# A new order of the four engines inside a quad of the attention, and wider column tiles in the recurrence's output matmuls

## The chip, the cores and the metric

The kernel runs on one core of a Trainium2 chip. The metric is the device time of one execution in microseconds (us). The kernel before takes 2658.96 us, the median of three runs (2658.64 to 2659.07).

## The reference

The program is one layer of a hybrid model on a stream of 2 x 2048 tokens with 256 features. It adds four blocks to the stream, each behind a layer norm:

```
x = x + attn_a(norm(x));  x = x + ffn(norm(x));  x = x + attn_b(norm(x));  x = x + ffn(norm(x))

# attn_a, 16 heads of 16 dims, segments of 64 tokens
scores = q k^T / 4, causal
out_t  = softmax(scores in the own and the previous segment) v        # the "window"
att    = softmax(scores)
pcs    = sum of att over the 64 rows of a segment, each row times exp(index_decay)
w      = decayed running sum of pcs over the segments before, divided by its sum + 1e-5
kv     = for each segment: sum over tokens s of  w[s] * k[s] (outer) v[s]
y      = sigmoid(mix) * out_t + (1 - sigmoid(mix)) * (q kv);   y @ Wc^T

# attn_b: tokens are routed to 2 of 4 memories (1024 tokens kept in each); a gated linear recurrence
# S = S * exp(g_t) + k_t v_t ;  o_t = q_t S   runs over each memory and over all tokens (shared)
# ffn: 16 experts, top 2, and a shared expert
```

## The kernel before, in words

The program is a row of phases. The change touches two: `phase_attend` (the softmax attention of attn_a, about 130 to 1240 us of the trace) and `phase_gla` (the recurrence of attn_b, about 1742 to 2292 us).

**phase_attend.** There are 2 x 16 = 32 heads (index n), and each head has 16 tiles of 128 query rows (t). A head is worked in four quads (q = 0 to 3) of four tiles: q, 7 - q, 8 + q and 15 - q; g = 4 n + q counts the quads, 128 in all. A quad's scores are made in units: unit 0 is the masked window (`window`, 768 columns), and units 1 to 4 or 1 to 5 are the causal score blocks (`scores(g, k)`), each up to 1024 columns in one of three PSUM buffers S. The quads q = 0 and q = 3 have four score units, q = 1 and q = 2 have five. Every unit goes through the engines in this order: TensorE writes S; VectorE takes the row minimum (`window_minima`, L725; `minima`, L737 and L740); ScalarE takes the exponential into SBUF (`window_exps`, L656; `exps`, L666). A fourth unit can only be written when the exponential of the first of the three has ended (TensorE's wait on `s_E`).

From the exponentials of quad g two chains run while the units of quad g + 1 are made.

- The window chain uses one PSUM bank M: TensorE turns the window (`turned`, L864); VectorE copies it to SBUF (`keep_transposed`, L757); TensorE multiplies it by v (`values`, L880); VectorE divides it and writes it to the stream (`outputs`, L764 and L767). Only then may M be written again.
- The share chain: GpSimd takes the difference of each block's minimum to the row's (`differences`, L556), ScalarE its exponential (`factors`, L673), GpSimd sums the window's diagonal part (`diag_sums`, L584 to L593) and the row totals (the first half of `weights`, L564 to L568), VectorE inverts them (`inverses`, L751), and GpSimd makes the shares c2 (the second half of `weights`, L570 and L576), in two buffers. TensorE uses c2(g) as stationary operand in `sums` (L887), which adds the column sums of quad g into the PSUM bank pcs in the next iteration.

Behind a head's last quad the sums of that head go on, spread over the next head's quads: ScalarE copies pcs to SBUF (`keep_pcs`, L679); TensorE turns it into M at the end of iteration q = 1 (`turn_pcs`, L922); ScalarE copies that (`keep_pcsT`, L685); TensorE multiplies it by the outer products kvo, in two halves (`products`, L933), one at the end of q = 2 and one behind the window of q = 3; ScalarE copies the result (`keep_kvr`, L691); TensorE applies the decay (`decayed`, L942), and VectorE normalises (`normalise`, L775 to L781). GpSimd makes kvo (`products`, L605) in parts of 5, 5 and 6 tiles in its iterations q = 3, 0 and 1. All of these use M too, so `turned` waits for `keep_pcsT` in q = 2, for `keep_kvr` in q = 3 and for `normalise` in q = 0.

Each engine's order is written out by hand: the loops over g at the end of each engine's block. An engine runs its list strictly in order, so an instruction that waits holds back all behind it.

**phase_gla.** 24 iterations of four chains of 128 tokens. TensorE computes the output of a pair of chains in `output(i, p)` (48 calls): for each of two chains a product of the queries with the state spread over 256 columns (`gl_bd`, L2670), and for each of four heads a product of the masked scores A with V, 64 columns (L2675). Both are cut into strips of output rows, `STRIP = P // 4 = 32` rows, so that the four strips lie in the four column groups of the array and their records (two for each f32 product) start nearly together.

Of the kernel before, what the change touches and what calls it, by code (L numbers as in the profile page):

```python
# [13 lines left out]
P = 128  # L14
# [3 lines left out]
NT = L // P  # L18
# [401 lines left out]
NQ = 4  # L420
# [5 lines left out]
def phase_attend(nc, q_parts, k_parts, k_tok, v_tok, tw, eid, decay, sq, sk, kh, vh, vs, ident, identb, mask, Y, kv_dram, x, q_full, wc, kvc,  # L426
                 q0, x0, wc_s, own, state, keep):

    with ExitStack() as ctx:
# [3 lines left out]
        NHEAD = B * H  # L433
        NG = NHEAD * NQ
# [111 lines left out]
        def _(pool):  # L546
# [7 lines left out]
            def differences(g):  # L554
                pool.wait_ge(s_top, g + 1)
                pool.tensor_tensor(diff[:, g % 2, :, :], mn[:, g % NQ, :, :],  # L556
                                   top[:, g % 2, :].unsqueeze(2).to_broadcast([P, NQ, KK]), ALU.subtract
                                   ).then_inc(s_diff, 1)

            def weights(g):  # L560
                q = g % NQ
                pool.wait_ge(s_f, g + 1)
                pool.wait_ge(s_ds, g + 1)
                pool.tensor_tensor(fr[:, :, :], f[:, q, :, :], rs[:, q, :, :], ALU.mult).then_inc(s_w, 1)  # L564
                pool.wait_ge(s_w, 3 * g + 1)
                pool.tensor_tensor(tot2[:, :], fr[:, :, 0], fr[:, :, 1], ALU.add).then_inc(s_w, 1)
                pool.wait_ge(s_w, 3 * g + 2)
                pool.tensor_tensor(tot[:, g % 2, :], tot2[:, :], fr[:, :, 2], ALU.add).then_inc(s_tot, 1)  # L568
                pool.wait_ge(s_inv, g + 1)
                pool.tensor_tensor(fi[:, :, :], f[:, q, :, :], inv[:, g % 2, :].unsqueeze(2).to_broadcast([P, NQ, KK]),  # L570
                                   ALU.mult).then_inc(s_w, 1)
                pool.wait_ge(s_w, 3 * g + 3)
                if g >= 2:
                    pool.wait_ge(s_P, g - 1)
                h = g // NQ % H
                pool.tensor_tensor(c2[:, g % 2, :, :, PAD:PAD + 2],  # L576
                                   fi[:, :, :].unsqueeze(3).to_broadcast([P, NQ, KK, 2]),
                                   eid[:, h, :].unsqueeze(1).unsqueeze(1).to_broadcast([P, NQ, KK, 2]),
                                   ALU.mult).then_inc(s_c2, 1)
# [32 lines left out]
            diag_sums(0)  # L612
            for g in range(NG):
                n, q = divmod(g, NQ)
                weights(g)
                if q == 3:
                    products(n, 0, 5)
                elif n and q == 0:
                    products(n - 1, 5, 10)
                elif n and q == 1:  # L620
                    products(n - 1, 10, NT)
                if g + 1 < NG:
                    differences(g + 1)
                    diag_sums(g + 1)
            products(NHEAD - 1, 5, NT)
            pool.memset(own[:, :, :], 1.0).then_inc(s_own, 1)
            pool.wait_ge(s_own, 1)
# [17 lines left out]
        def _(act):  # L645
# [50 lines left out]
            for g in range(NG):  # L696
                n, q = divmod(g, NQ)
                if g + 1 < NG:
                    window_exps(g + 1)
                    if n and q == 3:  # L700
                        keep_kvr(n - 1)
                    last = len(units[(g + 1) % NQ])
                    for k in range(1, 1 + last):
                        exps(g + 1, k)
                        if k == 1:
                            factors(g)
                        if n and k == 4 and q == 0:
                            keep_pcs(n - 1)
                        if n and k == 5 and q == 1:
                            keep_pcsT(n - 1)  # L710
            keep_kvr(NHEAD - 2)
            factors(NG - 1)
            keep_pcs(NHEAD - 1)
            keep_pcsT(NHEAD - 1)
# [3 lines left out]
        def _(dve):  # L718
# [68 lines left out]
            for g in range(NG):  # L787
                n, q = divmod(g, NQ)
                if g + 1 == NG:
                    inverses(g)  # L790
                    keep_transposed(g)
                    outputs(g)
                    if n:
                        normalise(n - 1)
                    break
                window_minima(g + 1)
                for k in range(1, 1 + len(units[(g + 1) % NQ])):
                    minima(g + 1, k)
                    if k == 2:
                        keep_transposed(g)  # L800
                    if k == 3:
                        inverses(g)
                        outputs(g)
                tops(g + 1)
                if n and q == 3:
                    normalise(n - 1)
            dve.wait_ge(s_keep, 1)
            normalise(NHEAD - 1)

# [1 line left out]
        def _(pe):  # L811
# [111 lines left out]
                                               start=True, stop=True)  # L923
                ins.then_inc(s_pT, 1)

            def products(n, part):
                if part == 0:
                    pe.wait_ge(s_pTs, n + 1)
                    pe.wait_ge(s_kvo, n + 1)
                    pe.wait_ge(s_Y, min(n * NQ + NQ + 3, NG))  # L930
                for t in range(part * NT // 2, (part + 1) * NT // 2):
                    j = t % 4
                    ins = nc.tensor.matmul(M[j * R:(j + 1) * R, 0:KVW],  # L933
                                           pcsT[:, t // 4 * P + j * R:t // 4 * P + (j + 1) * R], kvo[:, t, :],
                                           start=(t < 4), stop=(t >= NT - 4))
                if part == 1:
                    ins.then_inc(s_KV, 1)

            def decayed(n):
                pe.wait_ge(s_kvr, n + 1)  # L940
# [3 lines left out]
            window(0)  # L944
            for k in range(1, 1 + len(units[0])):
                scores(0, k)
            def next_sums(g, s, parts):
                if g >= 1:
                    sums(g - 1, s, parts)

            def next_scores(g, k):
                if g + 1 < NG and k <= len(units[(g + 1) % NQ]):
# [2 lines left out]
            for g in range(NG):  # L955
                n, q = divmod(g, NQ)
                if g + 1 < NG:
                    window(g + 1)
                if n and q == 3:
                    products(n - 1, 1)  # L960
                next_sums(g, 0, (0, 1))
                next_scores(g, 1)
                turned(g)
                next_scores(g, 2)
                next_sums(g, 1, (0, 1))
                next_sums(g, 2, (0,))
                next_scores(g, 3)
                values(g)
                next_sums(g, 2, (1,))
                next_scores(g, 4)  # L970
                next_sums(g, 3, (0, 1))
                next_scores(g, 5)
                if n and q == 1:
                    turn_pcs(n - 1)
                if n and q == 2:
                    products(n - 1, 0)
                if n and q == 3:
                    decayed(n - 1)
            for s, parts in ((0, (0, 1)), (1, (0, 1)), (2, (0, 1)), (3, (0, 1))):
                sums(NG - 1, s, parts)  # L980
            turn_pcs(NHEAD - 1)
            products(NHEAD - 1, 0)
            products(NHEAD - 1, 1)
            decayed(NHEAD - 1)


# [1055 lines left out]
def phase_gla(nc, gx, hT_dram, wq, wk, wv, w12, bg, yb, o_dram, ident, later, won, wo, nw):  # L2042

    with ExitStack() as ctx:
# [2 lines left out]
        UP = U * P  # L2047
        BK = 64
        BH = BK // 2
        STRIP = P // 4  # L2050
        NCHUNK = CAP // P
        NG = NCHUNK * (B + 1)
        NSTATE = B * NM + B
# [1019 lines left out]
```

## Time and profile before

| | us |
|---|---|
| median of 3 runs | 2658.96 |
| the profiled execution | 2684.99 |
| its span | 2683.3 |
| TensorE matmul busy | 2124.7 (79%) |
| VectorE busy | 1836.9 (68%) |
| ScalarE busy | 1561.9 (58%) |
| GpSimd busy | 1531.6 (57%) |

The profiled execution is 1.0% longer than the median of the runs. Busy times are those of the whole program; the phases have different limits, so the rows below take one phase or one head at a time. A line of the trace gives start, duration, engine, line of the kernel and operation, and in square brackets how long the engine had been idle and what released it. The duration of a block of matmuls includes the tail of its last record, which overlaps the next block.

### The profile page before, as it was taken

Reading aid. Unit: us, or ns where it says so; the run is one execution under the profiler, and the core shown is the slowest. Engines: PE = TensorE matmul, PEld = TensorE weight load, DVE = VectorE, ACT = ScalarE, POOL = GpSimd, SP = SyncE. Lnnn points to the kernel's source line nnn. Section 1 sums busy time; section 2 is a strip of 40 time slices with the busy share of each in tenths; the row PEclk is TensorE's granted clock in tenths of the full one; section 3 lists DMA queues with packets and bytes.
Section 4 is the critical chain, followed back from the end, with each engine's and each line's share of the span. In section 5 each row is a group of like instructions: output and inputs, shape, how many; then the busy total and the mean of one; then the engine's idle time right before and its main releaser. Section 6 shows DMA issues by size and latency. Waiting matters only on the chain. (4 is left out here: it accounts for less than half of the span.)

```text
span 2683.3 us, 111106 instructions
## 1 busy us (share of the span) xinstructions
PE 2124.7 (79%) x45872; PEld 1600.7 (60%) x45872; DVE 1836.9 (68%) x4507; ACT 1561.9 (58%) x3824; POOL 1531.6 (57%) x3168
## 2 busy tenths in 40 slices
PE   8788888888888888888868944389999998687793
PEld 5456566566566665556637734366766776565682
DVE  6578888887878887884544555276777777575456
ACT  5577777777777777772433322266666665454231
POOL 3357666666766666768554546544444444256452
PEclk9889999999999999999988965699999999789897
DMA  6911111111121111113346654301111111542546
GB/s 216 265 33 40 40 40 40 40 40 40 41 63 39 40 40 40 40 29 120 138 113 209 197 172 153 109 22 47 51 50 51 49 41 35 199 169 89 154 146 225
DMA packets 188851, 245.89 MB, mean 92 GB/s; under 512 B 41672, under 2 KB 144981, under 8 KB 187456
## 3 DMA queue, kind: packets, MB, share of 16 engines
q1 hardware_dynamic: 161824, 182.08, 22.7%
q0 software_dynamic: 19872, 50.41, 5.5%
q8 instruction: 368, 6.03, 0.9%
q10 hardware_dynamic: 6656, 6.31, 0.8%
q14 instruction: 131, 1.07, 0.1%
HBM read 136.08 MB, written 106.50 MB: 90 GB/s over the span
## 5 line engine op out<-in xcount | busy, mean ns | idle before, releaser
L666 ACT ACTIVATE at_E<-at_S,at_mn 128x1024 f32<-128x1024 f32 (+7 forms) x704 | 594.2, 847 | 211.3 <-DVE at_mn L737 178.2
L737 DVE TENSOR_REDUCE at_mn<-at_S 128x1 f32<-128x1024 f32 (+3 forms) x448 | 494.0, 1104 | 152.6 <-PE at_S L846 152.3
L846 PE MATMUL at_S<-am_sk,am_sq 96*32 96x512 bf16 (+3 forms) x4608 | 395.8, 350 | 1.1 <-ACT at_Tt L656 1.0
L887 PE MATMUL at_pcs<-at_E,at_c 128*32 128x256 f32 (+1 forms) x4864 | 375.7, 338 | 0.0
L605 POOL TENSOR_TENSOR at_kvo<-am_kh,am_vh 128x256 f32<-128x256 f32 x512 | 304.2, 628 | 0.0
L887 PEld LDWEIGHTS at_pcs<-at_E,at_c 128*32 128x32 f32 x4864 | 229.7, 109 | 41.2 <-issue 0.2
L1360 POOL DMA_INDIRECT expert_out<-m_ysb,m_dst x158 | 155.5, 984 | 139.3 <-issue 76.7
L887 PE MATMUL at_pcs<-at_Tt,at_c 128*32 128x128 f32 x1024 | 189.8, 274 | 42.3 <-ACT at_pcs_s L679 42.3
L590 POOL TENSOR_TENSOR at_half<-at_half 128x128 f32<-128x128 f32 (+4 forms) x640 | 185.6, 290 | 50.1
L864 PE MATMUL at_M<-am_ident,at_Tt 128*32 128x64 f32 x8192 | 154.5, 225 | 68.9 <-ACT at_kvr L691 43.1
L656 ACT ACTIVATE at_Tt<-at_S,at_mn 128x192 f32<-128x192 f32 x512 | 174.1, 428 | 48.3 <-DVE at_mn L725 48.1
L864 PEld LDWEIGHTS at_M<-am_ident,at_Tt 128*32 128x32 f32 x8192 | 136.3, 112 | 109.0 <-ACT at_Tt L656 54.8
L846 PEld LDWEIGHTS at_S<-am_sk,am_sq 96*32 96x32 bf16 x4608 | 173.8, 97 | 28.8 <-ACT at_Tt L656 10.3
L1672 PE MATMUL m_b<-m_wgu,m_xT 128*128 x632 | 169.1, 391 | 2.3 <-issue 2.0
L2609 PEld LDWEIGHTS gl_S<-gl_X,gl_Y 32*64 32x64 f32 x8448 | 110.5, 133 | 89.3 <-issue 68.9
L2609 PE MATMUL gl_S<-gl_X,gl_Y 32*64 32x32 f32 (+1 forms) x8448 | 132.0, 226 | 38.5 <-issue 24.3
L725 DVE TENSOR_REDUCE at_mn<-at_S 128x4 f32<-128x768 f32 x128 | 121.8, 951 | 34.6 <-PE at_S L829 34.4
L1413 ACT ACTIVATE m_sg<-m_b 128x128 f32<-128x128 f32 x158 | 43.9, 278 | 172.8 <-issue 105.9
L666 ACT ACTIVATION_READ_ACCUMULATOR at_E<-at_S,at_mn 128x1 f32 x704 | 143.0, 203 | 0.0
L887 PEld LDWEIGHTS at_pcs<-at_Tt,at_c 128*32 128x32 f32 x1024 | 107.0, 110 | 60.0 <-issue 48.7
L1672 PEld LDWEIGHTS m_b<-m_wgu,m_xT 128*128 128x128 f32 x632 | 120.2, 195 | 26.0 <-issue 9.9
L2241 POOL DMA_INDIRECT expert_out<-gl_ysb,gl_dst x64 | 64.8, 1013 | 109.7 <-ACT gl_ysb L2357 97.5
(393 smaller groups left out, 5579.9 us busy)
## 6 DMA issues: line engine op xcount, KB each, us to landing
m_xg<-expert_rows SPq DMA_DIRECT2D x158, 129.0 KB
am_sq<-q_parts SPq DMA_DIRECT2D x192, 64.0 KB, 2.3
am_sk<-k_parts SPq DMA_DIRECT2D x192, 64.0 KB, 2.3
memory_rows<-m_blank SPq DMA_DIRECT2D x16, 516.0 KB
gl_hx<-memory_rows SPq DMA_DIRECT2D x32, 258.0 KB, 3.6
m_wgu<-in_f_wgu SPq DMA_DIRECT2D x2, 4096.0 KB
rt_yin<-expert_out SPq DMA_DIRECT2D x7, 1024.0 KB, 11.4
fn_yin<-expert_out SPq DMA_DIRECT2D x7, 1024.0 KB, 8.9
```

The source lines that it names most:

```text
L590: pool.tensor_tensor(half[:, :, 0:w], half[:, :, 0:w], half[:, :, w:2 * w], ALU.add).then_inc(s_half, 1)
L605: ins = pool.tensor_tensor(kvo[:, t, 0:DH * DH].rearrange("p (d e) -> p d e", d=DH), k3[:, t, :].unsqueeze(2).to_broadcast([P, DH, DH]), v ...
L656: ins = nc.scalar.activation(Tt[:, q, s, :], S[v % NS_B][:, at:at + TW], ACT.Exp, bias=mn[:, q, s, 0:1], scale=-1.0)
L666: ins = nc.scalar.activation(E[:, at:at + w], S[v % NS_B][:, i * CW:i * CW + w], ACT.Exp, bias=mn[:, q, s, 1 + j:2 + j], scale=-1.0, accum ...
L725: nc.vector.tensor_reduce(mn[:, g % NQ, :, 0].rearrange("p (b s) -> p b s", b=2), S[v % NS_B][:, :].rearrange("p (b c) -> p b c", b=2)[:, ...
L737: nc.vector.tensor_reduce(mn[:, q, :, :].rearrange("p s k -> p (s k)")[:, at[0]:at[0] + 1], S[v % NS_B][:, 0:w], AX.X, ALU.min).then_inc(s ...
L846: ins = nc.tensor.matmul(S[v % NS_B][x, at:at + cw], sq[:, u, t * P + x.start:t * P + x.stop], sk[:, u, c0 + c:c0 + c + cw], start=True, s ...
L864: ins = nc.tensor.matmul(M[x, s * P + e * SEG:s * P + (e + 1) * SEG], Tt[:, q, s, e * SEG + x.start:e * SEG + x.stop], ident[:, e * SEG:(e ...
L887: ins = nc.tensor.matmul(pcs[j * R:(j + 1) * R, cols[0]:cols[1]].rearrange("p (b c) -> p b c", c=P), lhsT, rhs, start=(n, j) not in touche ...
L1360: pool.indirect_dma_start(out=yb.rearrange("t (j d) -> (t j) d", j=TOPK), out_offset=bass.IndirectOffsetOnAxis(ap=dst[:, t, :], axis=0), i ...
L1672: ins = nc.tensor.matmul(bank[4 + t % 2][:, 0:2 * MH], xT[:, t % 2, k, :], wgu[:, k, ds(at, D)], start=(k == 0), stop=(k == KC - 1))
L2609: return nc.tensor.matmul(out, Y[r_h, i % 2, l, u * P + keys:u * P + keys + out.shape[0]], queries, start=True, stop=True)
```

## The change

On GpSimd `weights` is cut in two, `totals` and `shares`. The order of an iteration g was weights(g), products, differences(g + 1), diag_sums(g + 1); it becomes totals(g), diag_sums(g + 1), shares(g), differences(g + 1), products.

On ScalarE `factors(g)` comes before the first score unit instead of behind it; `keep_pcs` comes behind the last unit of q = 0 instead of the fourth, `keep_pcsT` behind the fourth of q = 1 instead of the fifth, and `keep_kvr` behind the last unit of q = 2 instead of behind the window of q = 3.

On VectorE `keep_transposed` comes behind unit 1 instead of 2, `inverses` behind unit 4 instead of 3, and `normalise` behind unit 4 of q = 3 instead of behind `tops`.

On TensorE the sums of quad g - 1 move back: s = 0 from before `scores(g + 1, 1)` to behind `scores(g + 1, 2)`, s = 1 from there to behind `values`, and the second part of s = 3 to the next iteration, behind its window. `products` is one block of 16 tiles at the end of q = 2, and `decayed` comes before a fifth unit (q = 3 has none).

In `phase_gla` STRIP is 64 instead of 32.

```diff
@@ GpSimd
+            def shares(g):
+                q = g % NQ
                 pool.wait_ge(s_inv, g + 1)
...
-                weights(g)
+                totals(g)
+                if g + 1 < NG:
+                    diag_sums(g + 1)
+                shares(g)
+                if g + 1 < NG:
+                    differences(g + 1)
                 if q == 3:
                     products(n, 0, 5)
...
-                if g + 1 < NG:
-                    differences(g + 1)
-                    diag_sums(g + 1)
@@ ScalarE
                     window_exps(g + 1)
-                    if n and q == 3:
-                        keep_kvr(n - 1)
+                    factors(g)
                     last = len(units[(g + 1) % NQ])
                     for k in range(1, 1 + last):
                         exps(g + 1, k)
-                        if k == 1:
-                            factors(g)
-                        if n and k == 4 and q == 0:
+                        if n and k == last and q == 0:
                             keep_pcs(n - 1)
-                        if n and k == 5 and q == 1:
+                        if n and k == 4 and q == 1:
                             keep_pcsT(n - 1)
+                        if n and k == last and q == 2:
+                            keep_kvr(n - 1)
@@ VectorE
-                    if k == 2:
+                    if k == 1:
                         keep_transposed(g)
                     if k == 3:
+                        outputs(g)
+                    if k == 4:
                         inverses(g)
-                        outputs(g)
+                    if n and k == 4 and q == 3:
+                        normalise(n - 1)
                 tops(g + 1)
-                if n and q == 3:
-                    normalise(n - 1)
@@ TensorE
                     window(g + 1)
-                if n and q == 3:
-                    products(n - 1, 1)
-                next_sums(g, 0, (0, 1))
+                sums_of(g - 2, 3, (1,))
                 next_scores(g, 1)
                 turned(g)
                 next_scores(g, 2)
-                next_sums(g, 1, (0, 1))
-                next_sums(g, 2, (0,))
+                sums_of(g - 1, 0, (0, 1))
+                sums_of(g - 1, 2, (0,))
                 next_scores(g, 3)
                 values(g)
-                next_sums(g, 2, (1,))
+                sums_of(g - 1, 1, (0, 1))
+                sums_of(g - 1, 2, (1,))
                 next_scores(g, 4)
-                next_sums(g, 3, (0, 1))
+                sums_of(g - 1, 3, (0,))
+                if n and q == 3:
+                    decayed(n - 1)
                 next_scores(g, 5)
                 if n and q == 1:
                     turn_pcs(n - 1)
                 if n and q == 2:
-                    products(n - 1, 0)
-                if n and q == 3:
-                    decayed(n - 1)
+                    products(n - 1)
@@ phase_gla
-        STRIP = P // 4
+        STRIP = P // 2
```

## Rows read from the trace of the kernel before

**Rows 1.** Busy time of each engine in the attention and in the recurrence.
```profile
core 0: us, PE busy (x) PEld busy (x) DVE busy (x) ACT busy (x) POOL busy (x), PEclk, DMA share, GB/s
130.00:1240.00 1110.00, 906.41 (x27968) 663.54 (x27968) 881.14 (x1569) 841.23 (x2144) 764.35 (x2188) 0.98 0.16 40
1742.00:2292.00 550.00, 494.77 (x14190) 376.97 (x14188) 398.12 (x868) 356.37 (x678) 261.12 (x388) 0.98 0.14 43
```
**Rows 2.** Waits of TensorE in the attention: total us, times, longest.
```profile
PE at_M L880 <- DVE at_TTs L757: 71.9, 127, 1.6
PE at_M L864 <- ACT at_kvr L691: 43.1, 31, 1.4
PE at_pcs L887 <- ACT at_pcs_s L679: 42.3, 31, 2.2
PE at_M L864 <- ACT at_pcsT L685: 20.4, 31, 1.0
```
**Rows 3.** Busy time in TensorE's iterations q = 3, 0, 1, 2 of a head, and summed.
```profile
706.03:715.02 8.99, 6.98 (x221) 5.07 (x214) 5.97 (x12) 6.11 (x15) 3.67 (x14) 1.00 0.01 4
715.02:722.78 7.76, 6.58 (x217) 4.64 (x216) 7.32 (x15) 6.23 (x15) 6.62 (x19) 1.00 0.32 75
722.78:731.60 8.82, 7.03 (x233) 5.34 (x236) 7.29 (x14) 6.97 (x19) 7.22 (x20) 1.00 0.13 33
731.60:739.80 8.20, 7.03 (x220) 5.14 (x215) 6.92 (x12) 6.96 (x20) 6.13 (x18) 1.00 0.22 54
sum 33.77, PE 27.61 PEld 20.18 DVE 27.50 ACT 26.27 POOL 23.64; mean PE 27.61 PEld 20.18 DVE 27.50 ACT 26.27 POOL 23.64
```
**Rows 4.** TensorE in order of time, that head.
```profile
706.03 0.35 PE L822 MATMUL at_S<-am_mask,am_identb 128*32 128x384 bf16 x4
...
706.67 1.06 PE L933 MATMUL at_M<-at_kvo,at_pcsT 128*32 128x257 f32 x16
...
709.74 1.10 PE L864 MATMUL at_M<-am_ident,at_Tt 128*32 128x64 f32 x64 [1.42 <-ACT at_kvr L691]
710.63 0.64 PE L846 MATMUL at_S<-am_sk,am_sq 96*32 96x512 bf16 x8
...
724.99 0.27 PE L887 MATMUL at_pcs<-at_Tt,at_c 128*32 128x128 f32 x1 [1.36 <-ACT at_pcs_s L679]
...
730.73 1.08 PE L922 MATMUL at_M<-am_ident,at_pcs_s 128*32 128x128 f32 x32
```
**Rows 5.** VectorE in order of time, that head.
```profile
711.32 1.23 DVE L737 TENSOR_REDUCE at_mn<-at_S 128x1 f32<-128x1024 f32 x1 [1.84 <-PE at_S L846]
712.46 0.68 DVE L757 COPY at_TTs<-at_M 128x512 f32<-128x512 f32 x1
...
714.46 0.41 DVE L767 SCALAR_TENSOR_TENSOR stream<-at_M,am_gate,at_inv_t 128x32 f32<-128x32 f32 x2
...
716.34 0.47 DVE L781 TENSOR_SCALAR at_kvn<-at_M,at_rden 32x256 f32<-32x256 f32 x1
```
**Rows 6.** ScalarE in order of time, that head.
```profile
717.77 1.36 ACT L656 ACTIVATE at_Tt<-at_S,at_mn 128x192 f32<-128x192 f32 x4 [0.77 <-DVE at_mn L725]
...
721.52 1.11 ACT L666 ACTIVATE at_E<-at_S,at_mn 128x1024 f32<-128x1024 f32 x1 [0.31 <-DVE at_mn L737]
...
724.27 0.58 ACT L679 COPY at_pcs_s<-at_pcs 128x512 f32<-128x512 f32 x1
```
**Rows 7.** GpSimd in order of time, that head.
```profile
717.99 0.73 POOL L584 TENSOR_TENSOR at_half<-at_Tt 128x256 f32<-128x256 f32 x1
...
730.62 3.56 POOL L605 TENSOR_TENSOR at_kvo<-am_kh,am_vh 128x256 f32<-128x256 f32 x6
```
**Rows 8.** TensorE: recurrence outputs, 64-column tiles of another phase, bare weight loads.
```profile
1978.44 0.64 PE L2670 MATMUL gl_O<-gl_bd,gl_X 128*32 128x256 f32 x8
1978.87 0.66 PE L2675 MATMUL gl_O<-gl_V,gl_A 128*32 128x64 f32 x32
...
1283.47 1.09 PE L1129 MATMUL mg_lin<-am_state,mg_qT 128*64 128x128 f32 x16
...
1313.84 1.85 PE L1591 MATMUL m_b<-m_gw,m_hT 128*128 128x16 f32 x16
```

More of the change, by code:

```diff
@@ L558, in differences, with totals @@
                                    ).then_inc(s_diff, 1)
-            def weights(g):
+            def totals(g):
                 q = g % NQ
@@ L704, in _ @@
                         exps(g + 1, k)
-                        if k == 1:
-                            factors(g)
-                        if n and k == 4 and q == 0:
+                        if n and k == last and q == 0:
                             keep_pcs(n - 1)
-                        if n and k == 5 and q == 1:
+                        if n and k == 4 and q == 1:
                             keep_pcsT(n - 1)
-            keep_kvr(NHEAD - 2)
+                        if n and k == last and q == 2:
+                            keep_kvr(n - 1)
             factors(NG - 1)
@@ L924, in turn_pcs, with products @@
                 ins.then_inc(s_pT, 1)
[L926 to L931, printed above, removed]
+            def products(n):
+                pe.wait_ge(s_pTs, n + 1)
+                pe.wait_ge(s_kvo, n + 1)
+                pe.wait_ge(s_Y, min(n * NQ + NQ + 3, NG))
+                for t in range(NT):
                     j = t % 4
@@ L935, in products @@
                                            start=(t < 4), stop=(t >= NT - 4))
-                if part == 1:
-                    ins.then_inc(s_KV, 1)
+                ins.then_inc(s_KV, 1)
             def decayed(n):
@@ L946, in _, with sums_of @@
                 scores(0, k)
-            def next_sums(g, s, parts):
-                if g >= 1:
-                    sums(g - 1, s, parts)
+            def sums_of(g, s, parts):
+                if g >= 0:
+                    sums(g, s, parts)
             def next_scores(g, k):
@@ L975, in _ @@
                 if n and q == 2:
-                    products(n - 1, 0)
-                if n and q == 3:
-                    decayed(n - 1)
-            for s, parts in ((0, (0, 1)), (1, (0, 1)), (2, (0, 1)), (3, (0, 1))):
-                sums(NG - 1, s, parts)
+                    products(n - 1)
+            sums(NG - 2, 3, (1,))
+            for s in range(NQ):
+                sums(NG - 1, s, (0, 1))
             turn_pcs(NHEAD - 1)
-            products(NHEAD - 1, 0)
-            products(NHEAD - 1, 1)
+            products(NHEAD - 1)
             decayed(NHEAD - 1)
```

## The prediction

> **What bounds the kernel now.** I first read the busy time by stage. The attention is 1110 of the 2683 us; in it TensorE is busy 906 us, VectorE 881, ScalarE 841 and GpSimd 764 [rows 1]. None is full, so hand-offs set the time: each engine works its list in order, and each waits for the others in turn. The waits say where. TensorE, the fullest, waits 71.9 us for the turned window's copy (127 times), 43.1 for `keep_kvr`, 42.3 for `keep_pcs` and 20.4 for `keep_pcsT` (31 times each): 178 us in all, 5.7 per head [rows 2]. The busy times of one head say the same: 33.77 us long, TensorE 27.6, VectorE 27.5, ScalarE 26.3 and GpSimd 23.6 busy [rows 3]. The reader should see that the loss is uneven: iterations q = 3 and q = 1 take 8.99 and 8.82 us with 7 us of matmuls in them, q = 0 takes 7.76. In order of time the cause shows: `turned` of q = 3 starts after 1.42 us idle, released by the kvr copy, and the first sum of q = 1 after 1.36 us, released by the pcs copy [rows 4]. VectorE then stands 1.84 us, because the scores it needs are queued behind that `turned` [rows 5].
>
> **The change part by part: attention.** I lay the new order out by hand for one head. Lengths are the distance from a block to the next one, so a block's tail is taken off. TensorE: window 0.65 (706.03 to 706.67), `turned` 0.89 (709.74 to 710.63), `turn_pcs` 0.87, half of `products` 0.88 (both 1.07 without the 0.2 tail) [rows 4]; a 1024-column unit 0.43 (0.64 without tail), `values` 0.27 and a quad's sums about 2.5 to 2.6 (what is left of 27.6). VectorE: a 1024-column minimum 1.14 (711.32 to 712.46), the others by their columns, window 0.87; the TTs copy 0.60, `outputs` with its reciprocal 0.6, `normalise` 0.76 with its two small steps [rows 5]. ScalarE: window exponentials 1.22 without tail, 1024 columns 1.11, pcs copy 0.5 [rows 6]. A result is seen by the next engine 0.12 to 0.25 after its block. VectorE's own list is then 6.6, 6.6, 6.7 and 7.3 us for q = 0, 1, 2, 3.
>
> Take q = 0, and count from the issue of its first score block. TensorE: `turned` 0.4 to 1.3, unit 2 to 1.7, two sums to 2.5, unit 3 to 2.95, `values`. VectorE: window minimum ends 0.7, unit 1 (768 columns) 1.55, copy 1.55 to 2.15 (M is seen at 1.55), unit 2 to 3.3, unit 3 to 4.4. So unit 2, issued at 1.7, and `values`, whose copy is seen at 2.3, are both there in time: the 71.9 us of waits for TTs go. TensorE goes on with sums to 3.6, unit 4 to 4.3, sums to 4.9, unit 5 to 5.1. The next window needs unit 3's buffer: its exponential ends 1.4 after its minimum, at 5.85. The window is issued there and the first score block 1.1 later (window 0.65, the carried-over sums 0.43): the iteration takes 6.95. VectorE ends at 6.6 and loses 0.2.
>
> q = 1 adds `turn_pcs`, 5.15 to 6.0: 7.15. The pcs copy now stands behind unit 5 of the iteration before; it needs the carried-over sums, issued 1.1 after the window, and is done about 2 us before the first sum of head n, which has moved behind unit 2. So the 1.36 goes. `keep_pcsT`, a unit earlier, ends 0.2 before `turned` of q = 2: the 20.4 us go as well.
>
> q = 2: TensorE has 5.0 us of work, and then `products` waits for `outputs` (5.3), because these stand behind unit 3. It now runs 1.76 in one piece ahead of the next window, where half of it stood behind: 7.1, iteration 8.2. This edit costs: VectorE is done at 6.6 and the window minimum can start at 8.0, 1.4 us idle per head. What is bought is `keep_kvr`, which falls behind unit 4 of q = 2 and ends at 8.35, before `turned` of q = 3 at 8.55: the 43.1 us go.
>
> q = 3: TensorE could issue the next window at 5.7 (`decayed` waits for `outputs`, 5.3), but VectorE with `normalise` needs 7.3.
>
> The sum is 6.95 + 7.15 + 8.2 + 7.3 = 29.6 per head. Every short wait that I haven't seen comes on top; the same layout gives 6.95 for q = 0 of the kernel before, where VectorE's window minima stand 7.05 apart, and I add 0.15 per quad: 30.2. That is 3.5 less than 33.77, over 31 heads 109 us. The first head has nothing carried over and is left out, and so are the ends of the phase, which keep their work.
>
> GpSimd hides in this. Its five or six kvo tiles take 3.0 and 3.56 us, its diagonal sums 2.9 [rows 7], its list 7.4, 7.4, 8.0 and 4.5 us in q = 3, 0, 1, 2: 27.3, under 30.2. In its new order the totals come 4.2 to 5.7 us after `tops`, ahead of `inverses` at 6.1, so no wait there. The shares come 7.6 to 9.1 after `tops`; the first sum needs them at 9.0 to 10.0. Splitting `weights` adds no instruction. If that cover goes, c2 is late in q = 1 and 2 by what GpSimd is late, bounds 0 and 1 us per head; I take 0. The earlier `factors` needs `differences` at once, and has 2 us for it.
>
> **The change part by part: recurrence.** TensorE is busy 495 of 550 us there [rows 1]. A chain's output is 8 records of 256 columns (0.43 to the next block) and 32 of 64 columns (0.45) [rows 8]. That is two and eight rounds of four strips, each as long as one strip: 0.213 and 0.055. With 64-row strips a round holds two records and lasts as long, and the rounds stay two and eight: no gain from half the records. Nor is the pairing in doubt: in 128*64 tiles sixteen records of 128 columns take 1.09, less a tail of 0.27 that is 0.055 per record or 0.11 per pair, one record's own length [rows 8]. What is in doubt is the load. Sixteen records of 16 columns take 1.85, 0.11 each, which is a bare load of 128 columns [rows 8]; by halves 0.055 for 64 columns, as long as the 64-column record that must hide it. Bounds: 0 (hidden, or 0.03 gained per output by fewer records: -3 us over 96) and 0.055 more in each of the 10 rounds of 96 outputs (+53 us). The row nearest is that of the 128*64 tiles, where a load half as long as its record cost nothing; I take +3 us.
>
> The Trainium skill speaks against this edit: its page "TensorE: Matmul & The Clock Gate", Part 3, says that a weight load overlaps a running matmul only when its row group differs. These tiles all use 128 rows, so by it every load would show, and wider ones more. The 128*64 row above has 16 loads and shows none. By the rule the recurrence would lose about 27 us (the third rival).
>
> **Sum.** 2685 - 109 + 3 = 2579 for the profiled execution; it stood 1.0% over the runs' median, so 2659 - 105 = 2554, say 2555 us.
>
> **The rivals.**
> - *The waits move instead of going.* VectorE is nearly as full as TensorE [rows 3], and only the three copies' waits (105.8 us) [rows 2] are surely gone, while the undivided `products` gives back 0.88 and its wait for `outputs` another 0.3, 37 us, and small buffer waits 0.5 per head, 15 us. Gain 54: 2605 us. For it: three of four engines are above 26 us per head. Against: VectorE's idle time is mostly waits for scores stuck behind a stalled `turned`.
> - *The balance is better than I lay out.* If the carried lead absorbs the 1.4 us of q = 2, the head comes to 28.7, a gain of 157: 2505 us. For it: TensorE needs 27.6. Against: three buffers are a small lead.
> - *Wide loads show.* 0.028 (a 64-column load less a 32-column one) in 10 rounds of 96 outputs is 27 us; on the forecast: 2580 us.
> - *Slower: ScalarE held by its copies.* All three copies now wait, in order, for TensorE blocks issued just before: if TensorE runs late by d at `keep_pcs` or `keep_pcsT`, every exponential behind is late by d, the buffers stay full and TensorE is later still; `keep_pcs` even waits for work of the next iteration. It decides when the three stalls and the `products` block exceed the 4.1 us per head that the layout saves: a d of about 1.5 us each. At 1.8 each (5.4) the head is 1.3 longer, 40 us: 2700 us. For it: ScalarE has 26.3 of 33.8 us busy. Against: the layout gives d about 0.2.
> - *No net change*: at d of 1.3 to 1.4, about 2659 us.
>
> **How the numbers follow.** Forecast 0.60, waits move 0.18, better balance 0.07, wide loads 0.06, slower 0.06, no net change 0.03. Likeliest: 2555. The range reaches to the second case and past the first, 2500 to 2618. A measurement of this kernel tells 0.2%, 5 us, from no change: faster by more 0.91, within 0.03, slower 0.06.
>
> **What would show each step.** Right: in the attention TensorE's waits for TTs, kvr, pcs_s and pcsT fall from 178 us to under 40; `turned` of q = 3 and the first sum of q = 1 start without idle time; VectorE's largest wait is the window minimum behind `products`, about 1.4 us per head; a head is 30 us; `inverses` waits for GpSimd under 5 us. In the recurrence a chain's output still takes 0.43 and 0.45. Wrong: if TensorE waits for `outputs` or for ScalarE by over 2 us per head, if GpSimd's shares release the sums, or if the 64-column records start over 0.06 apart in pairs.

## The result and the profile after

The changed kernel takes 2509.55 us (median of 4 runs, 2505.94 to 2514.77) against 2659.02 us before (4 runs, 2658.64 to 2667.83): a ratio of 0.9438, with a 95% interval of 0.9419 to 0.9456. The forecast was 2555 us, its range 2500 to 2618. The gain is 149 us where 104 were forecast. The profiled execution took 2514.77 us (span 2513.1, mean granted clock 0.922; before 0.923), 0.2% above the median.

Busy times by stage, as in [rows 1]:

```profile
130.00:1095.00 965.00, 899.64 (x27968) 691.22 (x27968) 863.72 (x1569) 833.25 (x2144) 755.06 (x2188) 0.99 0.18 46
1590.00:2120.00 530.00, 492.12 (x12312) 384.51 (x12316) 393.81 (x862) 353.67 (x676) 261.65 (x389) 0.98 0.15 45
```

The work is the same (28.0 thousand matmul records and 900 us of TensorE in the attention), the stretch around it is 145 us shorter. From the first window's matmul to the last `decayed` the attention went from 1107.1 to 961.8 us. So the saving is idle time, and the waits of TensorE there must have gone. The view that answers to [rows 2] (total us, times, longest):

```profile
PE at_S L826 <- ACT at_E L671: 24.5, 34, 0.8
PE at_S L826 <- PEq L56: 16.7, 1, 16.7
PE at_M L868 <- issue: 5.6, 11, 0.8
PE at_M L944 <- DVE stream L770: 5.1, 22, 0.2
...
PE at_M L936 <- DVE stream L770: 2.6, 11, 0.4
...
PE at_M L926 <- ACT at_pcs_s L684: 0.7, 1, 0.7
PE at_M L868 <- ACT at_kvr L696: 0.5, 1, 0.5
```

The four waits of [rows 2], 178 us, are down to under 2 (those for `keep_transposed` and `keep_pcsT` have no row of a matmul any more). What is left per head is one wait of the next window for a free score buffer (0.8) and small ones for `outputs`; the 16.7 us of the second row are one wait at the start of the phase.

One head, in TensorE's iterations q = 3, 0, 1, 2, as in [rows 3]:

```profile
572.04:578.47 6.43, 6.42 (x207) 5.41 (x199) 5.30 (x9) 4.96 (x13) 2.78 (x10) 1.00 0.01 3
578.47:586.07 7.60, 6.78 (x214) 4.75 (x214) 7.50 (x16) 6.37 (x15) 6.30 (x18) 1.00 0.28 69
586.07:593.18 7.11, 6.71 (x226) 4.96 (x230) 6.82 (x15) 6.82 (x21) 6.41 (x19) 1.00 0.18 50
593.18:601.15 7.97, 7.93 (x240) 6.31 (x234) 7.24 (x13) 7.52 (x21) 7.19 (x21) 1.00 0.16 46
sum 29.11, PE 27.84 PEld 21.43 DVE 26.85 ACT 25.66 POOL 22.67; mean PE 6.96 PEld 5.36 DVE 6.71 ACT 6.42 POOL 5.67
```

TensorE idles 1.3 us of 29.1 where it idled 6.2 of 33.8. TensorE in order of time, that head (answers to [rows 4]):

```profile
573.49 0.28 PE L868 MATMUL at_M<-am_ident,at_Tt 128*32 128x64 f32 x4
573.59 1.21 PE L868 MATMUL at_M<-am_ident,at_Tt 128*32 128x64 f32 x60
...
578.63 0.38 PE L944 MATMUL at_M<-at_kvr,am_decay 128*32 128x257 f32 x1 [0.17 <-DVE stream L770]
...
586.24 0.35 PE L826 MATMUL at_S<-am_mask,am_identb 128*32 128x384 bf16 x4 [0.84 <-ACT at_E L671]
...
589.04 0.49 PE L891 MATMUL at_pcs<-at_Tt,at_c 128*32 128x128 f32 x3
...
592.49 1.08 PE L926 MATMUL at_M<-am_ident,at_pcs_s 128*32 128x128 f32 x32
...
599.64 1.94 PE L936 MATMUL at_M<-at_kvo,at_pcsT 128*32 128x257 f32 x32
```

`turned` of q = 3 (573.49) starts without the 1.42 us that it had before, the first sum of q = 1 (589.04) without the 1.36, and `products` is one block of 32 records, 1.94 us. VectorE in order of time shows the rhythm most clearly, because its window minimum opens every quad (answers to [rows 5]):

```profile
573.14 0.96 DVE L728 TENSOR_REDUCE at_mn<-at_S 128x4 f32<-128x768 f32 x1 [1.75 <-PE at_S L833]
...
580.29 0.94 DVE L728 TENSOR_REDUCE at_mn<-at_S 128x4 f32<-128x768 f32 x1
...
587.14 0.96 DVE L728 TENSOR_REDUCE at_mn<-at_S 128x4 f32<-128x768 f32 x1 [0.19 <-PE at_S L833]
...
594.27 0.96 DVE L728 TENSOR_REDUCE at_mn<-at_S 128x4 f32<-128x768 f32 x1 [0.34 <-PE at_S L833]
...
602.26 0.96 DVE L728 TENSOR_REDUCE at_mn<-at_S 128x4 f32<-128x768 f32 x1 [1.43 <-PE at_S L833]
```

The distances are 7.15, 6.85, 7.13 and 7.99 us; the 1.43 at the end is the wait behind `products`. Taken over 30 heads, the medians of these distances sum up the study (the last column is the median of whole heads and not the sum of the row); each is read from the starts of such lines. (Counted from TensorE's windows, as above, q = 3 and q = 0 take 6.43 and 7.60: TensorE issues the window early and pays it back in the buffer wait.)

| kernel | q = 3 | q = 0 | q = 1 | q = 2 | head |
|---|---|---|---|---|---|
| before | 9.82 | 7.06 | 8.72 | 8.23 | 33.83 |
| laid out in the prediction | 7.3 | 6.95 | 7.15 | 8.2 | 29.6 |
| changed | 7.16 | 6.85 | 7.14 | 8.00 | 29.49 |
| e3 copy behind unit 2 | 7.47 | 6.87 | 7.66 | 8.40 | 30.39 |
| e4 pcs copies in their old places | 7.16 | 6.85 | 7.26 | 8.39 | 29.81 |
| e5 halves of `products`, kvr copy in its old place | 9.27 | 6.85 | 7.14 | 7.16 | 30.66 |
| e6 GpSimd's old order | 7.15 | 7.34 | 7.92 | 8.67 | 31.08 |
| e7 sums in their old order | 7.16 | 6.85 | 8.80 | 7.98 | 31.24 |
| e8 halves of `products`, kvr copy in its new place | 7.97 | 6.85 | 7.13 | 7.14 | 29.32 |
| e9 no sums carried out of q = 0 | 7.16 | 6.85 | 7.13 | 8.02 | 29.31 |

In the recurrence, the rows that answer to the first two of [rows 8], and then the wait before weight loads of the score products (it was 68.9 us before; total, times, longest):

```profile
1849.78 0.66 PE L2677 MATMUL gl_O<-gl_V,gl_A 128*64 128x64 f32 x16
1850.25 0.63 PE L2672 MATMUL gl_O<-gl_bd,gl_X 128*64 128x256 f32 x4
1850.68 0.67 PE L2677 MATMUL gl_O<-gl_V,gl_A 128*64 128x64 f32 x16
```

```profile
PEld gl_S L2611 <- issue: 46.7, 72, 2.7
```

Half as many records take 0.43 and 0.47 us to the next block (medians over the phase: 0.453 for the state's product, 0.431 before; 0.464 for the product with V, 0.445 before). From its first transposed keys to its last product with V the phase went from 548.6 to 528.2 us in the two profiled executions, and what shrank lies outside these blocks.

### The profile page after: what moved, and what is told of

Its sections match the earlier page's. It is cut to its first block and busy times, and to the rows that moved or that the text cites. A ratio compares the mean times of both kernels' runs of the same rounds, so it can differ in the third digit from the quotient of the medians.

```text
span 2513.1 us, 107266 instructions
## 1 busy us (share of the span) xinstructions
PE 2097.4 (83%) x43952; PEld 1629.5 (65%) x43952; DVE 1817.8 (72%) x4507; ACT 1553.0 (62%) x3824; POOL 1521.3 (61%) x3168
## 5 line engine op out<-in xcount | busy, mean ns | idle before, releaser
L740 DVE TENSOR_REDUCE at_mn<-at_S 128x1 f32<-128x1024 f32 (+3 forms) x448 | 484.6, 1098 | 3.5 <-PE at_S L850 2.8
L891 PE MATMUL at_pcs<-at_E,at_c 128*32 128x256 f32 (+1 forms) x4864 | 409.3, 338 | 2.4 <-issue 2.3
L891 PEld LDWEIGHTS at_pcs<-at_E,at_c 128*32 128x32 f32 x4864 | 219.2, 109 | 20.5 <-issue 5.6
L850 PEld LDWEIGHTS at_S<-am_sk,am_sq 96*32 96x32 bf16 x4608 | 160.5, 97 | 72.0 <-ACT at_E L671 29.8
L891 PE MATMUL at_pcs<-at_Tt,at_c 128*32 128x128 f32 x1024 | 177.5, 274 | 0.6 <-issue 0.4
L728 DVE TENSOR_REDUCE at_mn<-at_S 128x4 f32<-128x768 f32 x128 | 122.1, 954 | 63.4 <-PE at_S L833 63.3
L2611 PEld LDWEIGHTS gl_S<-gl_X,gl_Y 32*64 32x64 f32 x8448 | 108.3, 132 | 67.5 <-issue 46.7
L2611 PE MATMUL gl_S<-gl_X,gl_Y 32*64 32x32 f32 (+1 forms) x8448 | 126.2, 226 | 22.3 <-ACT gl_A L2335 17.5
L826 PE MATMUL at_S<-am_mask,am_identb 128*32 128x384 bf16 x1024 | 99.7, 333 | 41.2 <-ACT at_E L671 24.5
L1666 PE MATMUL m_b<-m_ident,m_xg 128*128 128x128 f32 x316 | 62.2, 280 | 74.1 <-DMA m_xg<-expert_rows 74.1
```

The costliest lines, as they stand in the source:

```text
L728: nc.vector.tensor_reduce(mn[:, g % NQ, :, 0].rearrange("p (b s) -> p b s", b=2), S[v % NS_B][:, :].rearrange("p (b c) -> p b c", b=2)[:, ...
L740: nc.vector.tensor_reduce(mn[:, q, :, :].rearrange("p s k -> p (s k)")[:, at[0]:at[0] + 1], S[v % NS_B][:, 0:w], AX.X, ALU.min).then_inc(s ...
L850: ins = nc.tensor.matmul(S[v % NS_B][x, at:at + cw], sq[:, u, t * P + x.start:t * P + x.stop], sk[:, u, c0 + c:c0 + c + cw], start=True, s ...
L891: ins = nc.tensor.matmul(pcs[j * R:(j + 1) * R, cols[0]:cols[1]].rearrange("p (b c) -> p b c", c=P), lhsT, rhs, start=(n, j) not in touche ...
L2611: return nc.tensor.matmul(out, Y[r_h, i % 2, l, u * P + keys:u * P + keys + out.shape[0]], queries, start=True, stop=True)
```

## The experiments

Times of different sessions come from different chips (before: 2663, 2662 and 2684 us), so ratios are compared; 0.001 is 2.7 us.

**e1, the strips alone** (in the kernel before) **and e2, the attention alone** (in the changed kernel).

```diff
# e1, against before
-        STRIP = P // 4
+        STRIP = P // 2
# e2, against the changed kernel
-        STRIP = P // 2
+        STRIP = P // 4
```

> The kernel before with only the recurrence's strips at 64 rows; the attention is as before. Theory 1 (rounds, as predicted): the output blocks keep their length, the recurrence and the whole stay within 0.2% of the kernel before, 2656 to 2665 us. Rival (record supply): the recurrence lost its 20 us in the changed kernel's trace because 3840 fewer TensorE records have to be supplied, and the stretches of score matmuls stall less; then this kernel is 12 to 20 us faster than before, about 2642 us, with the output blocks unchanged and the idle time inside the score stretches (80 us in the trace of before) near 57 us. If the 20 us were only how that one profiled execution of before went, there is no gain in the timed runs.

> The changed kernel with 32-row strips in the recurrence again, so the attention's part of the change alone. Theory 1: all of the gain is here, 2510 us within 5 (ratio to before 0.944). Rival (record supply): 2525 to 2530 us, because the recurrence keeps its stalls; the attention stays 145 us shorter than before in either case.

e1: 2658.23 against 2663.35 us, ratio 0.9984 (0.9975 to 0.9994). e2: 2518.32 us, ratio 0.9462 (0.9449 to 0.9474). So the strips bring 4 us by e1 and some 6 by e2 (whose interval overlaps that of the changed kernel), and the attention 143. The rivals by which the wider strips cost something are out. Of the two expectations of e1 the first holds (within 0.2% of before) and the 12 to 20 us of the second don't; e2 came out between its two. The recurrence took 533.4 us in e2's profile and 528.6 in e1's, so most of the 20 us between the profiles of before and after was a long execution of before, 26 us over its median, and not the change; with 32-row strips in both, its recurrence is still 15 us longer than e2's.

**e3, the TTs copy back behind unit 2.**

```diff
-                    if k == 1:
+                    if k == 2:
                         keep_transposed(g)
```

> The changed kernel with the copy of the turned window behind unit 2 again on VectorE; all else changed. Theory 1 (early copy pays): values waits for the copy again, 0.4 to 0.6 us in most of the 128 quads, and outputs are no later, so the kernel loses 30 to 70 us against the changed one: 2540 to 2580. Rival (the copy only fills time that the buffers set): the exponential's buffer is what ends an iteration, TensorE has slack at values, and the loss is under 10 us: 2510 to 2520.

2552.04 us, ratio 0.9589 (0.9575 to 0.9603): 40 us slower than the changed kernel. Its waits in the attention:

```profile
PE at_M L884 <- DVE at_TTs L760: 86.7, 126, 1.5
ACT at_E L671 <- DVE at_mn L740: 67.0, 170, 1.4
```

The wait of before is back, and larger; less than half of it shows in the time. Part of it takes the place of another wait: TensorE's wait for a free score buffer before the next window, 24.5 us in the changed kernel, is down to 2.2. The largest wait of before is explained by the place of one copy.

**e4, the two pcs copies in their old places.**

```diff
-                        if n and k == last and q == 0:
+                        if n and k == 4 and q == 0:
                             keep_pcs(n - 1)
-                        if n and k == 4 and q == 1:
+                        if n and k == 5 and q == 1:
                             keep_pcsT(n - 1)
```

> The changed kernel with ScalarE's pcs copy behind the fourth unit of q = 0 and the pcsT copy behind the fifth of q = 1, as before; all else changed. Theory 1: the pcsT copy is late for turned of q = 2 by 0.5 to 0.9 us per head (15 to 30 us), and the pcs copy, now one unit early, holds ScalarE until TensorE's carried-over sums of the next iteration are done while a fifth unit waits behind it, 0.5 to 1 us per head (15 to 30 us): 2540 to 2565 us. Rival (three buffers absorb it): within 10 us of the changed kernel, 2510 to 2520.

2525.86 us, ratio 0.9486 (0.9472 to 0.95): 13 us slower, between the two expectations. One wait came back, and not that of the sums:

```profile
PE at_M L868 <- ACT at_pcsT L690: 12.1, 30, 0.4
```

So `keep_pcsT` had to move, worth its 0.4 us per head (q = 2 goes from 8.00 to 8.39). `keep_pcs` needed no move: the 42.3 us that TensorE waited for it in [rows 2] go because the first sum of q = 1 moved behind unit 2. e7 shows the other side of this.

**e5, `products` in two halves again, and the kvr copy behind the window of q = 3.**

```diff
                     window_exps(g + 1)
+                    if n and q == 3:
+                        keep_kvr(n - 1)
...
-                        if n and k == last and q == 2:
-                            keep_kvr(n - 1)
...
+                if n and q == 3:
+                    products(n - 1, 1)
                 sums_of(g - 2, 3, (1,))
...
-                    products(n - 1)
+                    products(n - 1, 0)
```

> The changed kernel with products in two halves around the window of q = 3 again and keep_kvr behind that window's exponentials, as before; all else changed. Theory 1: turned of q = 3 is ready 2.3 us after the window's issue and the kvr copy is done at 3.5, so 1.2 us of idle TensorE come back per head, less what the earlier window gives back to VectorE: 15 to 35 us more than the changed kernel, 2525 to 2545. Rival (VectorE's 1.4 us behind products costs as much as it buys): within 10 us of the changed kernel.

**e8, the halves alone, the kvr copy in its new place** (the third and fourth parts of the diff above; `products(n, part)` does half of the tiles).

> The changed kernel with products in two halves around the window of q = 3, but keep_kvr still behind the last unit of q = 2. Theory 1 (VectorE's idle time at that window is passed on): the window comes 0.88 us earlier, VectorE's wait there falls from 1.43 to about 0.6 us, and the buffer wait of TensorE at the end of q = 0 (0.83 us in the trace) mostly goes; the copy is done at 2.3 us, when turned is ready. Faster than the changed kernel by 15 to 30 us: 2480 to 2497. Rival (that idle time was free, TensorE's work is the bound): 2505 to 2515. Second rival: ScalarE stands at the copy until the second half is done and its window exponentials are late, 2520 to 2530.

e5: 2548.27 us, ratio 0.9574 (0.9558 to 0.9591), 36 us slower than the changed kernel, just over the 15 to 35 that were expected. e8: 2511.01 us, ratio 0.9445 (0.9429 to 0.9461), not to be told from the changed kernel: the 15 to 30 us of its first expectation didn't come, and its rival (that idle time was free) fits. Their waits, e5 first:

```profile
PE at_M L869 <- ACT at_kvr L696: 36.4, 31, 1.4
...
DVE at_mn L729 <- PE at_S L834: 37.3, 94, 1.0
...
DVE at_mn L741 <- PE at_S L851: 23.1, 34, 0.7
```

```profile
DVE at_mn L728 <- PE at_S L833: 36.8, 93, 1.0
...
DVE at_mn L740 <- PE at_S L850: 23.1, 35, 0.7
```

The first of these rows counts three windows per head; in the changed kernel it is 63.3 us, of which 44 stand behind `products`. In e8 19 of them are left there and 22 have appeared at unit 1 of q = 3: VectorE's idle is cut in two, moves (q = 2 and q = 3 take 7.14 and 7.97 instead of 8.00 and 7.16) and hardly gets less. What costs 36 us in e5 is the kvr copy alone. The undivided `products`, which the prediction charged with 1.4 us of VectorE's time per head, costs nothing that dividing it gives back in the timed runs; e8's attention is 4 us shorter in its one profile (957.9 against 961.8), which is as little as these runs can tell.

**e6, GpSimd's old order** (the totals and shares together behind the differences and diagonal sums of the iteration before, as one `weights`, VectorE's `inverses` where they are in the changed kernel).

```diff
                 totals(g)
-                if g + 1 < NG:
-                    diag_sums(g + 1)
                 shares(g)
-                if g + 1 < NG:
-                    differences(g + 1)
...
+                if g + 1 < NG:
+                    differences(g + 1)
+                    diag_sums(g + 1)
```

> The changed kernel with GpSimd's order as before (totals, shares, products, differences, diagonal sums); all else changed. Theory 1 (the order carries the gain): the differences come about 3 us after tops in three of four quads, factors, now ahead of the first unit, holds ScalarE about 1 us, and inverses waits for the totals 0.7 us or more: 2 to 4 us per head, 2570 to 2640. Rival (GpSimd is off the path): under 15 us, 2510 to 2525.

2560.74 us, ratio 0.9628 (0.9609 to 0.9648): 51 us slower, a little under what was expected.

```profile
DVE at_inv L753 <- POOL at_tot L568: 76.7, 94, 4.5
...
ACT at_f L677 <- POOL at_diff L556: 83.3, 93, 1.3
...
PE at_S L849 <- ACT at_E L670: 48.1, 76, 1.5
```

The `differences` come behind GpSimd's `products` in this order in three of four iterations (93 times in 31 heads); ScalarE's `factors`, which stand ahead of the first score unit, wait for them, and every exponential behind them is late; TensorE then waits for buffers. So the early `factors` and GpSimd's new order belong together: without the second, the first holds up ScalarE. How the 51 us divide between the late `totals` and the late `differences` isn't shown; the totals also wait for `factors`.

**e7, the sums of a quad in their old order** (the window's no longer split over two iterations).

```diff
-                sums_of(g - 2, 3, (1,))
+                sums_of(g - 1, 0, (0, 1))
                 next_scores(g, 1)
...
                 next_scores(g, 2)
-                sums_of(g - 1, 0, (0, 1))
+                sums_of(g - 1, 1, (0, 1))
                 sums_of(g - 1, 2, (0,))
...
-                sums_of(g - 1, 1, (0, 1))
                 sums_of(g - 1, 2, (1,))
                 next_scores(g, 4)
-                sums_of(g - 1, 3, (0,))
+                sums_of(g - 1, 3, (0, 1))
```

> The changed kernel with TensorE's sums in their old order (s = 0 ahead of the first unit, nothing carried over); all else changed. Theory 1: the shares of q = 0 and 1 are ready 1 to 1.4 us after TensorE asks for them, and 0.5 in the others, so the first sums wait and VectorE behind them: 1.5 to 3 us per head, 2555 to 2605. Rival (slack of the buffers hides it): under 15 us, 2510 to 2525.

2572.26 us, ratio 0.9663 (0.9645 to 0.9681): 60 us slower. The size was as expected, the reason was not:

```profile
PE at_pcs L891 <- ACT at_pcs_s L684: 49.8, 31, 1.6
...
PE at_pcs L891 <- POOL at_c L579: 12.0, 32, 1.1
```

Only 12 us are a wait for shares. Four times as much is the wait for the copy of pcs, once per head, in q = 1, which goes from 7.14 to 8.80. This is the 42.3 us of [rows 2] back, and more, since the copy stands one unit later than it did.

**e9, the carry out of q = 0 dropped, and e10, the same with the halves of e8.**

```diff
-                sums_of(g - 2, 3, (1,))
+                if q != 1:
+                    sums_of(g - 2, 3, (1,))
...
-                sums_of(g - 1, 3, (0,))
+                sums_of(g - 1, 3, (0, 1) if q == 0 else (0,))
```

> The changed kernel, but the second part of the sums of s = 3 is carried into the next iteration only in q = 1, 2 and 3; in q = 0 it stays ahead of the fifth unit, where TensorE waits 0.83 us for a buffer at the end of the iteration. Theory (TensorE's idle time is the only one that counts): 0.4 us of work falls into that wait, 0.4 us less per head, 13 us: 2495 to 2501. Rival (three buffers and VectorE's chain set the pace of q = 0 and 1): the next iteration's first unit comes earlier and finds no buffer or VectorE busy, under 5 us: 2505 to 2515.

> The same, with products in two halves around the window of q = 3 as well. Halves alone gave 4 us of attention in the profile and nothing that the timed runs could tell. Theory (idle time of TensorE alone counts, the two are independent): 2491 to 2499. Rival (with TensorE ahead in q = 1 and 2, VectorE's wait at the window of q = 3 decides again): 5 us or more better than the kernel without the halves.

2530.14 and 2533.37 us on a chip where before took 2684.17: ratios 0.9429 (0.9416 to 0.9442) and 0.9432 (0.9419 to 0.9445), not to be told from the changed kernel. The 13 us expected of e9 didn't come, nor the more expected of e10. e9's waits for buffers:

```profile
PE at_S L826 <- ACT at_E L671: 19.0, 33, 0.8
...
PE at_S L850 <- ACT at_E L671: 12.2, 33, 1.5
```

TensorE works where it waited at the window (24.5 to 19.0 us) and then waits a unit later (12.2 us, where the changed kernel has 1.3). So work put into this idle time of TensorE brings it no gain either. There was no better version among these.

**e11, one strip of 128 rows.**

```diff
-        STRIP = P // 2
+        STRIP = P
```

> The changed kernel with the recurrence's output strips at 128 rows: one column group, 8 records of 64 columns and 2 of 256 per chain. Theory (a weight load hides behind a record as long as itself and shows where it is longer): the 256-column records still take 0.43 us; the 64-column ones are paced by the load of 128 columns, 0.11 each as in the bare loads of rows 8, 0.9 us instead of 0.45, 96 times 0.4 = 40 us more: 2545 to 2555. Rival (fewer records pay more than the loads cost): under 15 us more, 2510 to 2525. If loads do not overlap at all in one row group, the 256-column block is longer too, 0.65 us, and the total 2565 or more.

2559.24 us on the chip of e9 and e10, ratio 0.9527 (0.9511 to 0.9542), so 24 us slower than the changed kernel and 26 to 29 slower than its neighbours there; 36 to 46 were expected. TensorE in order of time:

```profile
1791.76 0.67 PE L2672 MATMUL gl_O<-gl_bd,gl_X 128*128 128x256 f32 x2
1792.27 1.00 PE L2677 MATMUL gl_O<-gl_V,gl_A 128*128 128x64 f32 x8
```

Eight records of 64 columns take 0.84 us to the next block, 0.11 each, which is the bare 128-column load of [rows 8], as expected; the two records of 256 columns take 0.51 where the changed kernel takes 0.45, and 0.43 was expected. A load of 128 columns shows behind a record of 64 and hardly behind one of 256. By these distances the 96 outputs are 41 us longer than e9's, the recurrence is 24 (569.4 against 545.1): 17 are given back in other stretches, and this is what the expectation missed.

## Why the prediction came out as it did

**Right: what bounds the kernel, and what the change does to it.** The four waits went, and each of e3, e4, e5 and e7 brings one back by undoing one part. `turned` of q = 3 and the first sum of q = 1 start at once. VectorE's largest wait is the window minimum behind `products`, 1.75 and 1.43 us in the lines shown, 44 us over 31 heads, where 1.4 per head was laid out. `inverses` waits once for GpSimd, 2.5 us in the whole phase. Iteration by iteration the layout was 0.14, 0.10, 0.01 and 0.20 us too long (the table).

**Too small: the gain per head.** The measured 2509.55 us lies 45 us under the forecast and 10 over the lower end of the range. The attention gained 145 us where the sum had 109. The mean head is 29.55 us: 29.12 in an undisturbed head (9 of the 28 from 219 us on are within 0.03 of that) and 0.43 of disturbances, whose causes weren't looked into. Two terms were off, both the same way. The layout's 29.6 was 0.48 too long for an undisturbed head, 15 us over 31 heads; the table shows it in q = 2, q = 3 and q = 0. And "I add 0.15 per quad: 30.2" put 0.6 on top where the disturbances are 0.43, 5 us more. That 29.6 alone would have met the mean head is luck: the excess of the layout is as large as the disturbances that it leaves out. The addition was derived from 7.05 for q = 0 of before against 6.95 laid out, but that 0.1 was a property of the old order: in the new one q = 0 takes 6.85. A third term is the head of [rows 3], 33.77, while the mean of before was 34.0: 7 us over 31 heads. What remains, some 7 us, lies in the first head and the ends of the phase, and 2 us are rounding of 3.57 per head to 3.5.

**A part of the reasoning that experiments refuted.** The layout took VectorE's 1.4 us of idle at the end of q = 2 as a price of the undivided `products`. e8 takes half of it away there and gains nothing that the timed runs show, since the other half of `products` then stands before unit 1 of q = 3. The fullest engine is TensorE, 27.8 of 29.1 us, and what VectorE loses behind a block of TensorE's work is not lost twice. But TensorE's own 0.8 us of waiting for a buffer isn't bought back by filling it (e9), so the last 1.3 us per head aren't explained by TensorE's work alone, and no run here takes them away. The rival of a better balance put its price on this: the carried lead absorbs the 1.4, the head comes to 28.7 and the time to 2505 us. The time measured is nearest to that number, but not by that mechanism: the idle is still there, q = 2 takes 8.00 and not 6.8, and the difference to the forecast is the sum of the small terms above. That the time came out so near to this rival's is luck.

**The reason given for two parts.** The 1.36 us before the first sum of q = 1 went, as forecast, but the prediction let the moved copy and the moved sum share the credit; e4 and e7 give it to the sum alone. In fact the copy stands later than before, and only the moved sums make that harmless. Of GpSimd the prediction said that it hides in its new order, and it does; e6 gives the price if it didn't: 51 us, through `totals` that `inverses` waits for and `differences` that `factors` needs at once, a wait that the prediction named without a price.

**The rivals.** *The waits move*: the buffer wait that it priced at 0.5 per head came out at 0.8, the wait for `outputs` at 0.1 to 0.2 where it had 0.3, and the 0.88 of `products` wasn't given back (e8). *ScalarE held by its copies*: its d of 1.5 us didn't come; the copies of the changed kernel are waited for, by TensorE, under 2 us in all. It was a real danger elsewhere: e6 is a kernel in which ScalarE is held, by `factors`, and loses 1.6 us per head (31.08 against 29.49). *No net change* needed a d of 1.3 us and falls with it. *Wide loads*: below.

**The recurrence.** The block times moved by 0.022 and 0.019 us per output, over 96 outputs 4 us, where +3 was taken. But the phase got shorter: by 4 to 6 us in the timed runs of e1 and e2, and in the profiles of one chip it takes 528.6 us in e1 and 530.1 in e3 and e4, with 64-row strips, against 533.4 in e2, with 32-row strips. The missing term is outside the blocks. The wait before weight loads of the score products, in e1 and then in e2:

```profile
PEld gl_S L2609 <- issue: 48.6, 76, 2.7
PEld gl_S L2611 <- issue: 57.7, 79, 2.2
```

"issue" says that no engine's event ended it. The eight executions with 64-row strips outside the chip of e9 to e11 have 46.7 to 48.8 us of it, the two with 32-row strips 57.7 and 68.9. So this idle time gets less with the wider strips, though the blocks that they change lie elsewhere; between chips it differs as much (59.6 and 57.9 us in e9 and e10, with 64-row strips). That fewer records ahead of them let the following ones arrive in time would fit, but it was only argued. The term was off by 8 us, sign included.

The page "TensorE: Matmul & The Clock Gate" of the Trainium skill (Part 3) lets a weight load overlap a running matmul only when its row group differs, in its list of what overlaps; in the paragraph before that list it also lets a load into the background weight buffer go ahead. By the rule of the list, all loads here would show and those of 64 columns more than those of 32, by the prediction's estimate 27 us. The trace disagrees with that rule: with all 128 rows in use, the pairs of 64-column records with their 64-column loads still start 0.058 us apart (0.056 with 32-column loads before). Whether these loads go ahead by way of the background buffer no run here shows. e11 shows where a load does appear: one of 128 columns beside a record of 64.

## What to carry to other kernels

When no engine is full, write down for each iteration when every engine could start each step, and move the steps that sit ahead of what somebody else waits for; the layout from a few rows was good to 2% here (29.6 against 29.12 us), and its largest errors were small ones of 0.1 to 0.2 us per iteration that all went the same way. A step moved early on one engine needs its input moved early on another: the single undoings cost 40, 13, 36, 51 and 60 us, 200 in all where the whole is 143, so the parts depend on each other. Idle time of an engine that waits for the fullest one was no cost to be bought back here (e8).

## What was not expected of the hardware

- A column tile of 64 carries the same f32 work as two of 32 in nearly the same time (0.453 against 0.431 us for 4 and 8 records of 256 columns), while one of 128 is 1.8 times as slow for 64-column records (0.84 against 0.46).
- TensorE's gaps that no engine's event explains ("issue", before weight loads inside long rows of small matmuls) cost between 47 and 69 us in the recurrence, in executions of kernels with the same stretches: 46.7 in the changed kernel, 57.7 in e2, 68.9 before. The same recurrence took 528 us in the profiled execution on one chip and 545 on another.
